# A four-layer graph network on one Trainium2 core: gates of the target nodes applied to edge totals in layers 2 and 3, and a shared last node stage

## The reference

```
w = act(edge_scalars @ fc1) @ fc2          # per edge
m = w * (x[src] @ W1) * a[src] * edge_attr # per edge: 64+32 scalars, 64+32 vectors
agg = segment_sum(m, dst)
layer 0: cos(t)*sc + sin(t)*(agg @ W2)*a,  t = 0.1*(agg @ W3)*a
layer 1: sc + 0.5*(agg @ W2)*a
layer 2: n = agg/max(count,1);  sc + (n @ Wa)*a * (n @ W2)*a
layer 3: C_S*(x@Wa_sc*a + x@Wc_sc*c) + C_X*((agg @ Wa)*a*s + (agg @ Wc)*c*s)
```

## Time and profile before

| | |
|---|---|
| median of 3 runs | 4217.27 us |
| the profiled execution | 4216.08 us |
| its span, first to last instruction | 4214.4 us |
| busy: TensorE, its weight loads | 3591.9, 3337.9 us |
| busy: DVE, ACT, POOL | 2936.2, 2187.2, 2567.6 us |
| bytes moved | 682.78 MB, mean 162 GB/s |
| granted TensorE clock, mean | 0.935 |

### The profile page before, as it was taken

How to read it: one execution, slowest core, us unless ns; L and a number is a source line. 1 busy time by engine, 2 the same in 40 slices (tenths; PEclk the granted TensorE clock), 3 DMA queues, 4 the chain that set the end, 5 groups by cost and what they waited for, 6 DMA issues and landing times. The chain is left out here.

```text
span 4214.4 us, 104663 instructions
## 1 busy us (share of the span) xinstructions
PE 3591.9 (85%) x27044; PEld 3337.9 (79%) x27044; DVE 2936.2 (70%) x10747; ACT 2187.2 (52%) x5797; POOL 2567.6 (61%) x3126
## 2 busy tenths in 40 slices
PE   0699997666669999899989999899799999877676
PEld 0599996656569999877779999777699999866566
DVE  0577775888866666488856666688766666588888
ACT  0244443555544444377744444577655555477777
POOL 0377776777757777500057777444456666488887
PEclk9999998777779999999989999999999999988988
DMA  9522223666556555488832222588622222277775
GB/s 380 183 74 62 60 54 99 197 200 201 198 164 178 174 173 171 140 284 299 294 81 62 61 58 52 172 281 280 225 69 74 73 69 62 62 260 259 246 257 193
DMA packets 469538, 682.78 MB, mean 162 GB/s; under 512 B 212838, under 2 KB 285502, under 8 KB 465672
## 3 DMA queue, kind: packets, MB, share of 16 engines
q1 hardware_dynamic: 333546, 389.79, 30.2%
q0 software_dynamic: 75376, 125.21, 10.6%
q10 hardware_dynamic: 60512, 166.57, 10.0%
HBM read 391.37 MB, written 314.78 MB: 168 GB/s over the span
## 5 line engine op out<-in xcount | busy, mean ns | idle before, releaser
L537 POOL DMA_INDIRECT aggregates<-arena,meta x784 | 793.3, 1012 | 445.0 <-issue 240.8
L950 ACT ACTIVATE arena<-arena,shift,rstd 128x160 f32<-128x160 f32 x1600 | 697.2, 507 | 180.2 <-DVE shift L1210 177.7
L717 PE MATMUL bank<-same_all,msg 128*98 (+1 forms) x6272 | 753.4, 274 | 0.0
L528 POOL DMA_INDIRECT xg<-x_after,meta x588 | 575.9, 979 | 272.1 <-issue 251.0
L717 PEld LDWEIGHTS bank<-same_all,msg 128*98 128x98 f32 x6272 | 711.1, 166 | 0.0
L884 ACT ACTIVATE w<-bank 1x162 f32<-1x162 f32 (+1 forms) x784 | 257.2, 328 | 788.1 <-PE bank L750 782.2
L750 PE MATMUL bank<-w,arena 98*128 98x32 f32 (+1 forms) x4704 | 626.3, 270 | 0.0
L816 PEld LDWEIGHTS bank<-sc_cols,nT 128*128 128x128 f32 x2400 | 360.4, 221 | 290.2 <-issue 288.9
L750 PEld LDWEIGHTS bank<-w,arena 98*128 98x128 f32 x4704 | 588.0, 192 | 0.0
L1268 DVE SCALAR_TENSOR_TENSOR arena<-bank,attr,arena 128x160 f32<-128x160 f32 x1600 | 519.9, 378 | 88.3 <-PE bank L816 25.4
L816 PE MATMUL bank<-sc_cols,nT 128*128 128x128 f32 (+1 forms) x2400 | 373.0, 307 | 179.8 <-ACT nT L930 162.9
(11 more groups left out here) (142 smaller groups left out, 6832.0 us busy)
## 6 DMA issues: line engine op xcount, KB each, us to landing
arena<-aggregates SPq DMA_DIRECT2D x300, 324.0 KB, 4.3
x_after<-arena ACTq DMA_DIRECT2D x300, 320.0 KB, 3.6
arena<-x_after SPq DMA_DIRECT2D x300, 320.0 KB, 3.8
aggregates<-zeros SPq DMA_DIRECT2D x100, 640.0 KB
same_all<-aggregates SPq DMA_DIRECT2D x100, 640.0 KB, 5.2
aggregates<-same_all ACTq DMA_DIRECT2D x4, 8100.0 KB, 71.7
arena<-nodes SPq DMA_DIRECT2D x100, 320.0 KB, 3.1
out<-arena ACTq DMA_DIRECT2D x100, 320.0 KB, 3.9
```

What stands on the lines that cost most here:

```text
L528: gp.indirect_dma_start(xg[:, k % XGR, 4 + t * F:4 + (t + 1) * F], None, xtab[l], at).then_inc(gathered[k], 16)
L537: gp.indirect_dma_start(agg if l < 3 else agg3, at, tot[:, kk % TRING, t, 0:aw[l]], None, bounds_check=NP - 1, oob_is_err=False).then_inc( ...
L717: last = nc.tensor.matmul(bank[5 + t][0:MR, c * P:(c + 1) * P], msg[:, k2, t, c, :], same_all[:, bass.ds(here[t], P)], start=True, stop=True)
L950: last = nc.scalar.activation(row, row, ACT.Identity, bias=shift[:, kk, t:t + 1], scale=rstd[:, kk, t:t + 1])
```

## The change

- **Gates on the totals.** `meta_all` gets six more columns per pair, three per tile: 1/count squared times a, a*s and c*s of each edge's target. In E2 ACT first scales the total's column 0 (n @ Wa) by the first, waits for it, and scales the 160 columns by the product. In E3 ACT scales each group's 160 columns by its gate while it copies them to `tot`, DVE adds the two groups three steps behind, and POOL scatters 160 columns to the same table `agg`; `agg3` and its zero fills go.
- **Where the gates come from.** The count is made in E1 (column 1 of the totals) and kept by DVE per pair. In N1 POOL gathers, for each of the 98 pairs, the marks of the targets with two indirect DMAs of 16-byte rows from a new input, and keeps them four steps later; at the end of N1 DVE makes the gates in six operations on 196 columns (`dst_ready`), and SP's first loads of E2 wait for that.
- **N2** loses 1/count, the gates and the gating; TensorE waits for the load alone, as in N1.
- **N3.** POOL adds the aggregate to x in one operation. DVE multiplies and adds the self products of row sets 0 and 1 from banks 4 and 5 (4 instructions). ACT copies those of row sets 2 and 3 from banks 6 and 7 with the mark as scale into a ring `second` (4 instructions, one step behind), and POOL adds them in two operations. Statistics, square root, normalizing and store come one step later than before.
- **E3's f product**: four matmuls, each over both groups, for six.
- Small: radial inputs counted by 4 semaphores, not 8; xT and nT share memory; one more copy of the targets' indices in the prologue.

```diff
-APPLY_LAG = [4, 3, 3, 3]
-STORE_LAG = [5, 4, 4, 4]
+SQRT_LAG = [2, 2, 2, 3]
+APPLY_LAG = [4, 3, 3, 4]
+STORE_LAG = [5, 4, 4, 5]
 A_LEAD = 2
...
-    z3 = flat(agg3).rearrange("(c p n) -> c p n", c=NBLK, p=P)
-    def edge_loads_and_zeros(q, k, turn):
-        edge_loads(q, k, turn)
-        if l == 1 and within(q, 0, NBLK):
-            c = q if isinstance(q, int) else sp.snap(q)
-            sp.dma_start(z3[bass.ds(c, 1)].rearrange("o p (h n) -> (o p) h n", h=4), zeros[:, None, 0:AW3].to_broadcast([P, 4, AW3])).then_inc(zeroed3, 16)
-    steps(sp, 0, NBLK if l == 1 else NPAIR, EDGE_STEADY if l else FIRST_STEADY, edge_loads_and_zeros)
+    if l == 2:
+        sp.wait_ge(dst_ready, 1)
+    steps(sp, 0, NPAIR, EDGE_STEADY if l else FIRST_STEADY, edge_loads)
...
+    if l == 1:
+        sp.wait_ge(count_kept, NPAIR)
...
-            gp.wait_ge(tot_out, edge_count(l, q - 6))
+            if l < 3:
+                gp.wait_ge(tot_out, edge_count(l, q - 6))
+            else:
+                gp.wait_ge(tot_summed, q - 5)
...
+    def bring_marks(q, k, turn):
+        slot, use = k % XGR, turn * 2 + k // XGR
+        if within(q, XGR, NPAIR + XGR):
+            before = q - XGR if isinstance(q, int) else gp.snap(q - XGR)
+            gp.wait_ge(marks_in[slot], use * 32)
...
-            inv = pair_of(inv_count, k)[:, :, 1]
-            at = b + PC2
-            link(gp.tensor_tensor(g0, inv, inv, ALU.mult), at + 1)
-            link(gp.tensor_tensor(g1, g0, a0, ALU.mult), at + 2)
-            gp.tensor_tensor(g0, g1, pair_of(an, k)[:, :, :, 0], ALU.mult).then_inc(gates_ready, 2)
...
+            gp.tensor_copy(dst_marks[:, bass.ds(before, 1), :, :].rearrange("p o t c -> p (o t c)"),
+                           mark_ring[:, slot, :, :].rearrange("p t c -> p (t c)")).then_inc(marks_kept, 1)
+        if within(q, 0, NPAIR):
+            pair = q if isinstance(q, int) else gp.snap(q)
+            gp.tensor_copy(index_ring[:, slot, :], dst_index[:, bass.ds(pair, 1), :].rearrange("p o t -> p (o t)")).then_inc(index_ready, 1)
+            gp.wait_ge(index_ready, q + 1)
...
-            gp.tensor_tensor(g0, a0, a2, ALU.mult)
-            gp.tensor_tensor(g1, a1, a2, ALU.mult).then_inc(gates_ready, 2)
+            for t in range(2):
+                at = bass.IndirectOffsetOnAxis(ap=index_ring[:, slot, t:t + 1], axis=0)
+                gp.indirect_dma_start(mark_ring[:, slot, t, :], None, mark_rows, at).then_inc(marks_in[slot], 16)
...
+    def add_both(b, k, turn):
+        kk, tt = back(k, turn, 1, NRING)
+        if within(b, 0, NBLK):
+            gp.wait_ge(a_in[k], node_slot(l, k, turn) * 16)
+            gp.wait_ge(nturned, node_count(l, b))
+            alone(gp, passed["gp"])
+            x = xn[:, k].rearrange("p (t c) -> p t c", t=BT)
+            gp.tensor_tensor(x, x, an[:, k, :, 2:AW], ALU.add).then_inc(x_added, 1)
+        if within(b, 1, NBLK + 1):
+            gp.wait_ge(second_gated, b)
+            gp.wait_ge(x_added, b + NBLK)
+            alone(gp, passed["gp"])
+            x = xn[:, kk].rearrange("p (t c) -> p t c", t=BT)[:, 2:4]
+            gp.tensor_tensor(x, x, second[:, kk % XGR, 0:2], ALU.add).then_inc(first_added, 1)
+            gp.wait_ge(first_added, b)
+            alone(gp, passed["gp"])
+            gp.tensor_tensor(x, x, second[:, kk % XGR, 2:4], ALU.add).then_inc(second_added, 1)
+    def node_moves(b, k, turn):
+        if k % 2 == 0 and within(b, 0, NBLK):
+            make_gates(b, k, turn)
...
-        else:
-            gp.tensor_tensor(x, x, row, ALU.add).then_inc(first_added, 1)
-            gp.wait_ge(second_gated, b + 1)
-            gp.wait_ge(first_added, b + 1)
-            alone(gp, passed["gp"])
-            gp.tensor_tensor(x, x, an3[:, k, :, F:2 * F], ALU.add).then_inc(x_added, 1)
...
+        if l == 1:
+            bring_marks(b, k, turn)
+        if l == 3:
+            add_both(b, k, turn)
+    steps(gp, 0, NBLK + (0, NPAIR + XGR - NBLK, 0, 1)[l], NODE_STEADY, node_moves, NRING)
...
-            for g in range(G):
+            if G == 1:
                 for c in range(3):
                     a, e = c * CH, min((c + 1) * CH, W1C)
-                    last = nc.tensor.matmul(bank[3 + g][:, a:e], xT[:, k2, c * P:(c + 1) * P],
-                                            w1[l][:, g * W1C + a:g * W1C + e], start=True, stop=True)
+                    last = nc.tensor.matmul(bank[3][:, a:e], xT[:, k2, c * P:(c + 1) * P], w1[l][:, a:e],
+                                            start=True, stop=True)
+            else:
+                both = lambda ap, a, e: ap.rearrange("p (g c) -> p g c", g=2)[:, :, a:e]
+                for c, t, a, e in ((0, 0, 0, 128), (1, 0, 128, 160), (1, 1, 0, 96), (2, 1, 96, 160)):
+                    last = nc.tensor.matmul(both(bank[3 + t][:, 0:2 * F], a, e), xT[:, k2, c * P:(c + 1) * P],
+                                            both(w1[l], t * F + a, t * F + e), start=True, stop=True)
...
-                if l == 1:
-                    pe.wait_ge(a_in[kk], node_slot(l, kk, tt) * 16)
-                else:
-                    pe.wait_ge(gated, b + NBLK)
+                pe.wait_ge(a_in[kk], node_slot(l, kk, tt) * 16)
...
-            wait(pe, y_stt, base - 3)
+            wait(pe, y_stt, base - 2)
...
-            wait(pe, y_stt, base - 2)
+            wait(pe, second_gated, b - 1)
...
-            last = nc.scalar.activation(tot[:, kk % TRING, t, 0:aw[l]], tb[t][:, 0:aw[l]], ACT.Copy)
+            if l == 1 and (not isinstance(q, int) or q >= 6):
+                act.wait_ge(count_kept, q - 5)
+            if l < 2:
+                last = nc.scalar.activation(tot[:, kk % TRING, t, 0:AW], tb[t][:, 0:AW], ACT.Copy)
+            elif l == 2:
+                nc.scalar.activation(of_extra[:, t:t + 1], tb[t][:, 0:1], ACT.Copy,
+                                     scale=meta[:, kk, 18 + 3 * t:19 + 3 * t]).then_inc(extra_gated, 1)
+                act.wait_ge(extra_gated, 2 * q - (2 + t))
+                alone(act, passed["act"])
+                last = nc.scalar.activation(tot[:, kk % TRING, t, 2:AW], tb[t][:, 2:AW], ACT.Copy,
+                                            scale=of_extra[:, t:t + 1])
+            else:
+                for g in range(2):
+                    last = nc.scalar.activation(tot[:, kk % TRING, t, 2 + g * F:2 + (g + 1) * F], tb[t][:, g * F:(g + 1) * F],
+                                                ACT.Copy, scale=meta[:, kk, 19 + 3 * t + g:20 + 3 * t + g])
...
-        if l == 3 and within(b, 0, NBLK):
-            act.wait_ge(gates_ready, b + (2 * NBLK + 1))
-            act.wait_ge(a_in[k], node_slot(l, k, turn) * 16)
+        if l == 3 and within(b, 1, NBLK + 1):
+            kk, tt = back(k, turn, 1, NRING)
+            wait(act, second_added, b + (1 - 1 - XGR))
+            act.wait_ge(attr_copied, node_count(l, b - 1))
+            act.wait_ge(sc_ready, 2 * (b + l * NBLK))
             alone(act, passed["act"])
-            for j in range(BT):
-                row = an3[:, k, j, F:2 * F]
-                last = nc.scalar.activation(row, row, ACT.Copy, scale=gates[:, k, j, 1:2])
+            for g in range(2):
+                for j in (2, 3):
+                    last = nc.scalar.activation(second[:, kk % XGR, 2 * g + j - 2, :], bank[4 + j][:, g * F:(g + 1) * F],
+                                                ACT.Copy, scale=attr[:, kk, j, g:g + 1])
             last.then_inc(second_gated, 1)
...
+nc.vector.tensor_copy(by_field(dst_index[:, :, :]), four(bank[3])[:, 0:2])
...
+        if l in (1, 3) and within(q, 3, NPAIR + 3):
+            kk, tt = back(k, turn, 3)
+            dve.wait_ge(tot_out, edge_count(l, q - 3))
+            if l == 1:
+                pair = (NPAIR + 2) - q
+                if not isinstance(q, int):
+                    pair = dve.snap(pair)
+                nc.vector.tensor_copy(dst_count[:, bass.ds(pair, 1), :].rearrange("p o t -> p (o t)"),
+                                      tot[:, kk % TRING, :, 1]).then_inc(count_kept, 1)
+            else:
+                dve.wait_ge(carried_tot, edge_count(l, q - 3))
+                alone(dve, passed["dve"])
+                nc.vector.tensor_tensor(tot[:, kk % TRING, :, 2:AW], tot[:, kk % TRING, :, 2:AW],
+                                        tot[:, kk % TRING, :, AW:AW + F], ALU.add).then_inc(tot_summed, 1)
...
-        nc.vector.tensor_scalar(top, an[:, k:k + 2, :, 1], 1.0, None, ALU.max).then_inc(count_max, 2)
-        dve.wait_ge(count_max, b + 2)
-        nc.vector.reciprocal(inv, top).then_inc(count_ready, 2)
...
+        late = 2 if l == 3 else 1
+        ki, ti = back(k, turn, late, NRING)
         def inverse():
-            if l and within(b, 1, NBLK + 1):
-                dve.wait_ge(std_ready, b + (l - 1) * NBLK)
-                nc.vector.reciprocal(rstd[:, kk, :], std[:, kk, :]).then_inc(rstd_ready, 1)
+            if l and within(b, late, NBLK + late):
+                dve.wait_ge(std_ready, b + ((l - 1) * NBLK + 1 - late))
```

(62 more changed lines are left out.)

172 lines of the change are left out of this document (83 added, 89 removed).

## The result

The changed kernel takes 4104.45 us, the median of 4 runs (4101.09 to 4108.37), beside 4215.60 of the kernel before (4 runs, 4213.63 to 4219.17; three of them are the ones given ahead of the prediction): a ratio of 0.9736 with a 95% interval of 0.9719 to 0.9753. The profiled execution has a span of 4098.9 us, 115.5 less than before.

What follows compares the result with a forecast made beforehand. It took TensorE to bound E1 to E3 and N1, DVE and POOL N3; stage terms summed to -73.5 us, 4142.6 from 4216.1, plus 1.2 to the median: 4144, own range 4120 to 4165, overall 4112 to 4182.

Steps and rivals of the forecast that it cites:

- ACT's step becomes 4.61 - 0.10 = 4.51 us and is the next bound: N3: four PSUM readings replace ACT's four gatings, 1.17 us for 1.27, and ACT then sets the step.
- -74.6 for -53: N3 term -53 us: -56 from the step falling from 5.15 to 4.58, +3 for a longer drain.
- 0.07 "for clock and late banks": N3: 0.07 us a step added to ACT's 4.51 for clock and late banks.
- My -56 us: N3: 99 steps falling from 5.15 to 4.58 us, before +3 for the drain.
- -23.4 for -21: N2 term -21 us: it becomes N1's code, 99 steps falling from 3.53 to 3.31 us.
- -14.1 for -7: E3 term: -8 us over 98 pairs from four f matmuls for six, and +1 at the end.
- Rival 4, the matmul count: E3's gain goes by number of matmuls, not columns: -35 us more, 4109; chance 0.06.
- +5, +2, 0 and +0.5: Terms in us: E2's total scaling +5, N1's mark gathers +2, E1's dropped fills 0, the prologue's extra copy +0.5.
- DVE as N3's bound: Rival 1, N3: POOL's additions hold up DVE's line 1238, DVE step 4.9 us, +32 us, 4176; chance 0.13.
- POOL at 3.8 in N1: Rival 2, N1: POOL needs 3.8 us a pair, stage and E2's start 30 us later, 4174; chance 0.08.
- The descriptors: Rival 3, N1: the marks' descriptors clog the DMA engines, stage 98 us longer, 4240; chance 0.03.
- N3 not freed: Rival 5, N3: the second half still reaches DVE through POOL and ACT, 53 us less gain, 4197; chance 0.02.

Runs made afterwards that it cites:

- one add in the wrong place: Kernel with N3's sharing undone plus one 640-column POOL add per step, released by DVE's products of the block before: N3 540.2 us.
- the same pass on DVE: Changed kernel with one of N3's four normalizing passes moved from ACT to DVE: N3 498.1 us; 418.2 with the store one block later.
- the kernel with the sharing undone: Changed kernel with DVE taking all eight N3 products, ACT reading no bank, POOL making one add, gates left on the totals: N3 472.2 us.

## Why the prediction was wrong, point by point

The spans fell by 115.5 us for a sum of 73.5. The 42 us between them are 22 in N3, 7 in E3, 4 in E2, 3 in N1, 2 in N2 and 3.5 in the stages up to N0, the last within what E0 alone varies by.

*N3, the step that failed.* "ACT's step becomes 4.61 - 0.10 = 4.51 us and is the next bound" was right in its mechanism (one activation more costs 28 us, an add on POOL nothing) and mis-sized; the stage came out 22 us below its term (-74.6 for -53). The step of 4.51 measured 4.40 (-11 us): four readings took 1.11 and not 1.17, the rest of the step shown 0.02 less than in the earlier trace rows, and the mean is 0.03 below that step. The 0.07 "for clock and late banks" was not needed: in the windows of 100 us between 3670 and 4070 the clock was granted at 1.00, where the earlier trace rows had 0.87, and no bank was late (-7 us). The drain took 0.9 us less and not 3 more (-4 us).

*What I had not seen in N3.* My -56 us rested on DVE's four products. Shared out, they were worth 19, because ACT was the next bound close by. The rest came of DVE's shift no longer meeting POOL's gating: 0.52 us a step. I had that meeting as a rival, as something that would stay. It stays, at 0.24 us: the shift's group has a mean of 386 ns, and all but a few of the stage's end with POOL's first add.

```profile
3854.99 0.86 POOL L651 TENSOR_TENSOR arena<-arena,same_all 128x320 f32<-128x320 f32 x1 [1.12 <-ACT same_all L974]
...
3855.48 0.39 DVE L1282 SCALAR_TENSOR_TENSOR shift<-mv,rstd 128x4 f32<-128x4 f32 x1
```

ACT's sqrt releases DVE and ACT's readings release POOL, and the two start 0.04 us apart (3854.95 and 3854.99), so the meeting is in every step at one place, never at its worst, and a DVE that idles 24.7 us in 100 for the sqrt pays it for nothing.

*N2.* -23.4 for -21, by comparing it with N1, which was the right way; the trace of the changed kernel has 3.29 us a step and N1 3.30. What was gone was for the most part not what I named first: 1/count is 7 us of it.

*E3.* -14.1 for -7. From the first f matmul to the first w matmul it took the 1.26 us that I had summed, but the next slot shrank as well (0.71 in the earlier trace rows, 0.65 here):

```profile
3300.47 1.42 PE L782 MATMUL bank<-weights,nT 128*128 128x256 f32 x8
...
3301.73 0.82 PE L790 MATMUL bank<-weights,arena 128*128 128x192 f32 x4
...
3302.38 0.39 PE L761 MATMUL bank<-w,arena 98*128 98x128 f32 x2
```

The period went from 6.25 to 6.12, and putting the six back costs 12. By columns I was right, by the size of the term 4 us short; why the second slot shrank was not tried. Rival 4, the matmul count, would have been 43.

*E2, N1, E1, prologue.* +5, +2, 0 and +0.5 measured +0.8, -1.1, -0.1 and, with E0 and N0, -3.0. The terms of E2 and N1 were a "might come late" that I rounded up. ACT had 0.38 us ahead of line 872, and the gate used that up and no more. The mark step on POOL is 3.34 us, 3.48 with the copy of the marks of a pair of blocks, 3.44 in the mean, against N1's 3.30; the last of 98 is kept at 2114, and the count's chain and SP's first loads behind it fit into what N1's end and E2's start took before: the stage is as long as before (-1.1 us).

*Rivals.* DVE as N3's bound: no, though the meeting of shift and POOL that it names was, once gone, the larger half of the gain. POOL at 3.8 in N1: no, 3.44. The descriptors: N1's DMA share is 0.90 with the marks' gathers and 0.86 without them, and twice the gathers are bound by POOL, not by them. N3 not freed: no.

*The range.* All seven terms came out at or above what was measured, so the errors were not independent. In N3, N1 and E2 I added allowances for which no row stood (0.07 a step, +3, +2, +5), 17 of the 40 us by which 4144 missed; the step of 4.51 in N3 and E3's second slot are most of the rest. The low end had only a part of one rival in it.

## What to carry to other kernels

Where a change frees several engines at once, the new step is one engine's list added up from start to start, its store issues included, as long as no ring of waits through several engines is longer; take it as measured and add nothing for what has no row. When an instruction is slow only now and then, look at what the neighbour was doing when it was issued: POOL busy 96 us in 100 cost 9 us in all, and one add in the wrong place 0.69 us a step. And when one engine stands near 100%, try the order within its list and who issues its transfers before moving arithmetic: the same pass on DVE was worth +45, -35, +6 or -10 us, by the waits around it.

## What the runs showed of the hardware

In two sessions the same kernel before takes 5046 and 5050 us and not 4214, and it is only the edge stages: E0 to E3 of the kernel with the sharing undone take 762, 777, 836 and 800 us beside 547, 567, 548 and 622 in another kernel with the same edge stages (two adds more on POOL), while N0, N1, N2 take 519, 351, 347 beside 519, 346, 345. 100 us of E2 there, and of the changed kernel's E2 in a session of the other kind:

```profile
2800.00:2900.00 100.00, 77.40 (x491) 70.70 (x492) 36.90 (x99) 32.15 (x100) 42.88 (x44) 0.79 0.15 36
```

```profile
2200.00:2300.00 100.00, 100.00 (x845) 95.23 (x843) 63.77 (x171) 53.04 (x168) 74.42 (x75) 1.00 0.25 64
```

The granted clock is 0.79 where it was 1.00 (of the two levels of 2.4 and 1.2 GHz, a mix), and TensorE has idle time besides: 491 matmuls in 100 us for 845, and the stage half as long again. In that E2 TensorE stands idle 23 times for 2 to 5.5 us, 97 us in all, where the kernel before and the changed one have no such pause. The stages that lengthen are those in which TensorE is busy 97 to 98% of the time otherwise. The cause was not tried, nor whether it is another chip or another condition of the same one: the record puts number 12 for the chip beside the session with 5046 us and beside the next one, with 4214. The changed kernel itself didn't run in these two sessions. The kernel with one add more on POOL, whose N3 is as long as the changed kernel's, has a ratio of 0.9822 there (0.9776 to 0.9868), where the changed kernel's is 0.9743 (0.9727 to 0.9759): a ratio from one kind of session doesn't hold in the other.
